# Two attention layers in one program: 64x64 tiles for the block layer's scores, norm scaling on GpSimd, sums of the full layer in halves

## What is computed

```python
# layer 1, block sparse: 16 blocks of 64 rows
q, k, v = (heads(x @ W.T + b) for each of Wq, Wk, Wv)
# block rows 0 and 15 attend to all 1024 keys; row 1 to blocks 0, 1, 2, 15; row 14 to 0, 13, 14, 15
# block rows i = 2..13 attend to blocks 0, i-1, i, i+1, 15
ctx = softmax(scores * scale) @ v
x = layernorm(x + ctx)
# layer 2, full attention, and a layer of 8 experts
hn = layernorm(x) * g1 + b1                  # q, k, v of hn; every row attends to all 1024 keys
x2 = x + (softmax(q @ k.T / sqrt(8)) @ v) @ wo + bo
hn2 = layernorm(x2) * g2 + b2
idx = argmax(hn2 @ gate_w + gate_b)          # one expert per row
x3 = x2 + (relu(hn2 @ w1[idx] + b1[idx]) @ w2[idx] + b2[idx])
out = layernorm(x + x3)
```

## Time and profile before

| what | us |
|---|---|
| median of 3 runs (lowest, highest) | 940.32 (936.14, 944.61) |
| the profiled execution's own time | 937.35 |
| its span, first to last instruction | 935.6 |
| TensorE busy | 762.3 |
| VectorE busy | 565.6 |
| ScalarE busy | 443.0 |
| GpSimd busy | 203.7 |

### The profile page before, as it was taken

The page is one execution under the profiler, slowest core; times in us unless marked ns, Lnnn a source line. Parts: engine busy times, 40 slices in busy tenths (PEclk is TensorE's granted clock), DMA queues, the critical chain, the costliest instruction groups (busy, mean ns, idle before and its releaser), DMA issues.

```text
span 935.6 us, 17249 instructions
## 1 busy us (share of the span) xinstructions
PE 762.3 (81%) x6594; PEld 343.4 (37%) x6594; DVE 565.6 (60%) x941; ACT 443.0 (47%) x826; POOL 203.7 (22%) x460
## 2 busy tenths in 40 slices
PE   4299999999999999977789999987999987305950
PEld 2135655556555565531122212131212122205950
DVE  3253344334554344579987899979789941623745
ACT  2024233333334334327767787866777886002621
POOL 5213420000223342011213410002100000063650
PEclk9557676658657776569989999999999999556985
DMA  4411111212111111111101111110111124013103
GB/s 120 67 18 19 19 19 19 26 19 30 19 19 19 19 19 19 19 15 18 17 10 17 18 22 22 26 14 11 16 18 20 18 78 126 0 40 87 34 32 90
DMA packets 28699, 28.88 MB, mean 31 GB/s; under 512 B 4592, under 2 KB 23824, under 8 KB 28624
## 3 DMA queue, kind: packets, MB, share of 16 engines
q1 hardware_dynamic: 27216, 24.96, 15.4%
q0 software_dynamic: 1408, 2.89, 0.9%
HBM read 9.35 MB, written 5.53 MB: 16 GB/s over the span
## 4 chain that ended last, share of the span: by engine, by line
PE 65%; DVE 18%; issue 5%; POOL 4%; ACT 4%; DMA 3%; SPq 1%; POOLq 0%; ACTq 0%; DVEq 0%
PE PO L1101 23%; PE RB L1138 22%; PE EX L1146 11%; DVE NM L874 11%; ACT PR L732 3%; PE EX L1058 2%; POOL sorted_rows L661 2%; PE RB L1190 1%; PE RB L1115 1%; POOL results L681 1%; PE EX L1197 1%; DVE ST L823 1%; DMA QKT<-QS 1%; PE RB L1089 1%; DVE X L843 1%
## 5 line engine op out<-in xcount | busy, mean ns | idle before, releaser
L874 DVE TENSOR_REDUCE NM<-RB 128x1 f32<-128x1024 f32 (+2 forms) x416 | 433.2, 1067 | 239.7 <-PE RB L1138 229.7
L732 ACT ACTIVATE PR<-EX 128x512 f32<-128x512 f32 (+1 forms) x736 | 383.1, 586 | 300.2 <-PE EX L1146 299.0
L1138 PE MATMUL RB<-QKT 48*128 48x512 bf16 (+4 forms) x1248 | 313.2, 339 | 55.8 <-DVE NM L874 35.5
L1146 PE MATMUL EX<-QKT 51*128 51x512 bf16 (+2 forms) x1536 | 305.6, 309 | 10.3 <-ACT PR L732 6.9
L1101 PE MATMUL PO<-PR,VB 128*32 128x512 f32 (+3 forms) x3072 | 253.1, 440 | 0.1
L1138 PEld LDWEIGHTS RB<-QKT 48*128 48x128 bf16 (+1 forms) x1248 | 94.0, 103 | 286.1 <-DVE NM L874 142.9
L1146 PEld LDWEIGHTS EX<-QKT 51*128 51x128 bf16 (+1 forms) x1536 | 99.4, 111 | 114.7 <-ACT PR L732 69.5
L1101 PEld LDWEIGHTS PO<-PR,VB 128*32 128x32 f32 x3072 | 94.6, 128 | 51.0 <-issue 35.8
L637 POOL COPY VB<-VST 128x128 f32<-128x128 f32 (+1 forms) x64 | 18.7, 292 | 340.4 <-PE PO L1101 327.7
L647 POOL CAST MS<-NM 128x16 bf16<-128x16 f32 x32 | 6.3, 198 | 169.3 <-DVE NM L874 142.0
L755 ACT COPY QS<-QS 128x1156 f32 x12 | 13.8, 1155 | 57.8 <-DVEq L965 43.1
(11 more groups left out here) (158 smaller groups left out, 510.7 us busy)
## 6 DMA issues: line engine op xcount, KB each, us to landing
QKT<-QS SPq DMA_DIRECT2D x64, 192.0 KB
QS<-in_L_ffn_w_dram SPq DMA_DIRECT2D x1, 2048.0 KB, 9.3
QS<-in_L_ffn_w_dram SPq DMA_DIRECT2D x4, 512.0 KB, 9.5
sorted_rows<-PR SPq DMA_DIRECT2D x3, 516.0 KB, 10.1
QKT<-sorted_rows SPq DMA_DIRECT2D x3, 516.0 KB, 5.6
QKT<-MT SPq DMA_DIRECT2D x64, 6.0 KB
CTX<-results SPq DMA_DIRECT2D x2, 512.0 KB, 5.1
X<-_attn_hidden_states_dram SPq DMA_DIRECT2D x2, 384.0 KB, 4.1
```

The lines of the kernel that those rows point to most:

```text
L732: nc.scalar.activation(PR[:, at % RING, h, 0:n], bank(key)[:, 0:n], ACT.Exp).then_inc(s_aread, 1)
L874: nc.vector.tensor_reduce(NM[v % 2][:, h, tiles[0]:tiles[-1] + 1], ps, AX_X, ALU.max, negate=True).then_inc(s_dread, 1)
L1138: ins = pe.matmul(spread(ps[r0:r1, c:c + of[1] * of[3]], of), columns(v, h, 0, ROWS6, (l0, 1, 0, ln)), columns(v, h, 1, ROWS6, of), start= ...
L1146: ins = pe.matmul(spread(ps[r0:r1, c:c + of[1] * of[3]], of), columns(xv, xh, 1, ROWS9, (l0, 1, 0, ln)), columns(xv, xh, 0, ROWS9, of), st ...
```

## The change

Four edits:
- In the block layer every score matmul that had a 128-column stationary operand becomes two of 64 columns, LOW and UPP, in both passes. The maxima's pieces are regrouped: `window` gives for each 64 rows the 128 columns of the outer blocks and then the near blocks, in one piece where they lie side by side.
- The last three AV groups of the block layer become one.
- In the full layer each AV group of 512 columns becomes two of 256, the first due one beat after its EXP step, the second (`late`) one more. Groups of the block layer are due at the later of the two.
- SCALE is done on GpSimd, in all norms but that of the second sequence ahead of the experts.

```diff
@@ full_layer
-    L.av_groups = [dict(last=2 * kt + 1,
-                        mms=[(h, a, 2 * kt + a, (0, 512), "full", kt, 0) for a in range(2) for h in range(2)])
-                   for kt in range(TT)]
+    L.av_groups = [dict(last=2 * kt + 1, late=half, mms=[(h, a, 2 * kt + a, (half * 256, 256), "full", kt, half * 256)
+                                                         for a in range(2) for h in range(2)])
+                   for kt in range(TT) for half in range(2)]
@@ block_layer
-    L.max_acts = [dict(tiles=(0,), n=1024, mms=[(ALL, k * 512, (0, P), (k * 512, 1, 0, 512)) for k in range(2)])]
+    def window(j, off, col):
+
+        blk, rows = 2 * j + off // BLK, UPP if off else LOW
+        query, c = (j * P + off, BLK), block_col(blk)
+        if j == TT - 1:
+            near = [(P, (block_col(13), 1, 0, P) if off == 0 else (block_col(2), 2, block_col(1) - block_col(2), BLK))]
+        elif block_col(blk - 1) == c - BLK:
+            near = [(P, (c - BLK, 1, 0, 3 * BLK))]
+        else:
+            near = [(P, (block_col(blk - 1), 1, 0, BLK)), (P + BLK, (c, 1, 0, 2 * BLK))]
+        return [(rows, col, query, (0, 1, 0, P))] + [(rows, col + c0, query, of) for c0, of in near]
+
+    def turns(f):
+
+        return [m for pair in zip_longest(f(0), f(BLK)) for m in pair if m]
+
+    L.max_acts = [dict(tiles=(0,), n=1024, mms=[(LOW if off == 0 else UPP, k * 512, (off, BLK), (k * 512, 1, 0, 512))
+                                                for k in range(2) for off in (0, BLK)])]
     for j in range(1, TT - 1, 2):
-        L.max_acts.append(dict(tiles=(j, j + 1), n=320, mms=[m for i in (0, 1) for m in [
-            (ALL, 512 * i, ((j + i) * P, P), (0, 2, (j + i) * P, P)),
-            (LOW, 512 * i + 2 * P, ((j + i) * P, BLK), (block_col(2 * (j + i) - 1), 1, 0, BLK)),
-            (UPP, 512 * i + 2 * P, ((j + i) * P + BLK, BLK), (block_col(2 * (j + i) + 2), 1, 0, BLK))]]))
+        L.max_acts.append(dict(tiles=(j, j + 1), n=320, mms=[m for i in (0, 1) for m in turns(
+            lambda off: window(j + i, off, 512 * i))]))
...
     L.exp_steps = [first[0], odd, first[1], even, own, rest, ends]
+    for st in L.exp_steps:
+        st["mms"] = [half for rows, c, (l0, ln), of in st["mms"] for half in
+                     ([(LOW, c, (l0, BLK), of), (UPP, c, (l0 + BLK, BLK), of)] if rows == ALL else [(rows, c, (l0, ln), of)])]
@@ plan
             for e in steps:
-                ready[e] = beats[i + 1] + 0.4
-        acts += [(ready[gr["last"]], 5, "AV", li, u, g) for g, gr in enumerate(L.av_groups)]
-        exp_end.append(ready[L.av_groups[-1]["last"]] + 0.2)
+                ready[e, 0], ready[e, 1] = beats[i + 1] + 0.4, beats[i + 2] + 0.4
+        acts += [(ready[gr["last"], gr.get("late", 1)], 5, "AV", li, u, g) for g, gr in enumerate(L.av_groups)]
+        exp_end.append(ready[L.av_groups[-1]["last"], 1] + 0.2)
@@ block.gpsimd
+                if kind == "SCALE" and (li, u) != (2, 1):
+                    src, dst = ((X, X1[:]), (X1, X[:]))[k[0]] if li == 1 else (X, HN2[:, :, 0:HS])
+                    for t in (2 * k[1], 2 * k[1] + 1):
+                        g = u * TT + t
+                        nc.gpsimd.tensor_scalar(dst[:, g, :], src[:, g, :], MV[:, t, 0:1], RD[:, t:t + 1],
+                                                ALU.subtract, ALU.mult).then_inc(s_norm, 1)
@@ block.vector
-                if kind == "SCALE":
-                    n, src, dst = 2 * u + k[0], (X, X1)[k[0]], (X1, X)[k[0]]
...
-                    if (li, u) != (2, 1):
-                        dve.wait_ge(s_newton, 4 * ROOT_STEPS * (n + 1))
-                    elif k[1] == 0:
+                if kind == "SCALE" and (li, u) == (2, 1):
+                    n = 4 + u
+                    if k[1] == 0:
```

More of the change, by code:

```diff
@@ L1 @@
 from contextlib import ExitStack
+from itertools import zip_longest
 import numpy as np
@@ L87, in block_layer @@
     t7 = (TT - 1) * P
-    L.max_acts = [dict(tiles=(0,), n=1024, mms=[(ALL, k * 512, (0, P), (k * 512, 1, 0, 512)) for k in range(2)])]
-    for j in range(1, TT - 1, 2):
-        L.max_acts.append(dict(tiles=(j, j + 1), n=320, mms=[m for i in (0, 1) for m in [
-            (ALL, 512 * i, ((j + i) * P, P), (0, 2, (j + i) * P, P)),
-            (LOW, 512 * i + 2 * P, ((j + i) * P, BLK), (block_col(2 * (j + i) - 1), 1, 0, BLK)),
-            (UPP, 512 * i + 2 * P, ((j + i) * P + BLK, BLK), (block_col(2 * (j + i) + 2), 1, 0, BLK))]]))
[L94 to L97, removed]
+    def window(j, off, col):
[12 more added lines that the diff above has]
+                                                for k in range(2) for off in (0, BLK)])]
+    for j in range(1, TT - 1, 2):
+        L.max_acts.append(dict(tiles=(j, j + 1), n=320, mms=[m for i in (0, 1) for m in turns(
+            lambda off: window(j + i, off, 512 * i))]))
+    L.max_acts.append(dict(tiles=(TT - 1,), n=256, mms=turns(lambda off: window(TT - 1, off, 0))))
     def single(j, col):
@@ L137, in block_layer @@
                                          (h, 0, 3, (0, 384), "full", 0, P)])),
[L138 to L143, removed]
+        dict(last=6, mms=both(lambda h: [(h, j % 2, 4, ((j - 1) * P, P), "full", j, j // 2 * P) for j in range(1, 5)]) +
+             both(lambda h: [(h, j % 2, 5, ((j - 5) * P, P), "full", j, j // 2 * P) for j in (5, 6)] +
+                  [x for a, b_ in ((1, 2), (3, 4))
+                   for pair in zip(single_v(h, 5, a, 2 * P + (a - 1) * BLK),
+                                   single_v(h, 5, b_, 2 * P + (b_ - 1) * BLK)) for x in pair]) +
+             both(lambda h: [x for pair in zip(single_v(h, 6, 5, 0), single_v(h, 6, 6, BLK)) for x in pair]))]
     L.kinds = ["full", "low", "upp"]
@@ L416, in av_group_of @@
         def av_group_of(li, e):
-            return [i for i, gr in enumerate(LAYERS[li].av_groups) if gr["last"] >= e][0]
+            return max(i for i, gr in enumerate(LAYERS[li].av_groups) if any(m[2] == e for m in gr["mms"]))
         def piece(li, b, k):
@@ L830, in do @@
                         root_guess(VE[:, 0:TT], RD[:, 0:TT], SD[:, 0:TT]).then_inc(s_var, 1)
-                if kind == "SCALE":
-                    n, src, dst = 2 * u + k[0], (X, X1)[k[0]], (X1, X)[k[0]]
-                    if li == 2:
-                        n, dst = 4 + u, HN2[:, :, 0:HS]
-                    if (li, u) != (2, 1):
-                        dve.wait_ge(s_newton, 4 * ROOT_STEPS * (n + 1))
-                    elif k[1] == 0:
+                if kind == "SCALE" and (li, u) == (2, 1):
+                    n = 4 + u
+                    if k[1] == 0:
                         dve.wait_ge(s_var, n + 1)
@@ L842, in do @@
                         g = u * TT + t
-                        nc.vector.tensor_scalar(dst[:, g, :], src[:, g, :], MV[:, t, 0:1], RD[:, t:t + 1],
+                        nc.vector.tensor_scalar(HN2[:, g, 0:HS], X[:, g, :], MV[:, t, 0:1], RD[:, t:t + 1],
                                                 ALU.subtract, ALU.mult).then_inc(s_norm, 1)
```

## The result

The changed kernel takes 844.14 us (median of 4 runs, 832.37 to 847.26) against 938.39 us before (4 runs); the ratio is 0.892 with a 95% interval of 0.879 to 0.904. Predicted were 863 us, 808 to 908. The profiled execution took 847.26 us with a span of 845.5. All ratios here leave out runs that count as slow: of the changed kernel 845.24 and the profiled 847.26, and elsewhere, among others, one run of the kernel before of 1377.76 us and two of e10 of 1802 us, which nothing here explains.

What follows compares the result with a forecast made beforehand. TensorE was taken to bound the block layer and VectorE the full layer. 937.35 - 64 (block layer units) - 3.5 (first unit) - 6 (scaling) = 863.9, said as 863 us, range 808 to 908.

Steps and rivals of the forecast that it cites:

- each turn costs: Block layer scores: full-width and half-width stationary shapes taking turns cost 0.22 us; ten turns are most of a 2.4 us beat.
- Halves run side by side: Block layer scores: low and high 64x64 halves overlap, 0.053 us for both together, at most some 0.026 a pair.
- Beats 3 and 4: Block layer, two maximum steps with exponent scores: 1.0 us each plus 0.4 for MT, 5.24 becomes 2.4, saving 2.8.
- Beats 5 to 8: Block layer: they wait for VectorE's reduces, 2.95 us to beat 9, where they and the sums took 4.61.
- over 16 units: Block layer: each unit falls from 20.9 to 16.9 us, 4.0 saved, 64 us over all 16 units.
- rival B: Block layer: denser stream raises the clock, units of about 12.5 to 13 us, 802 us in all; chance 0.20.
- C: Block layer: thin waits for VectorE lower the clock, 19.4 us a unit, 905 us in all; chance 0.17.
- I take 0: Full layer, sums by halves: 31 us of TensorE switches hidden behind reduces, net 0, bounds -10 to +31 us.
- Scaling, 6 us saved: Norms: 24 scalings in the full layer's time leave VectorE for GpSimd, 6 us saved, bounds 0 and 9.
- D: Full layer becomes TensorE's: the 31 us of switches land in full, 894 us; chance 0.06.
- E: Block layer: halves don't run side by side in long streams, columns double, about 940 us; chance 0.04.
- F: Block layer: 64-column weight loads come one after another, 0.11 us a pair, +4.9 us a unit, 1015 us; chance 0.05.

Runs made afterwards that it cites:

- e10: The kernel before with only the loads of q and k due 9 ahead of their unit in place of 6; 945.15 us, ratio 1.004.
- e1: The kernel before with the block layer's 64x64 score tiles alone, sums, due times and scaling as before; 876.74 us, ratio 0.934.
- e11: e5 with the block layer's maxima pieces as before the change (18 of 46 a unit with 128 columns), exponent's in 64x64; 912.25 us, ratio 0.975.
- e5: The changed kernel with the loads of q and k due 9 before their unit in place of 6; 820.38 us, beside 936.39 for the kernel before.
- e9: The changed kernel with the early loads and each block-layer score step's pieces ordered low halves first, then high ones; 816.36 us, ratio 0.868.
- e3: The kernel before with the full layer's sums in halves alone, due one beat and two after their exponents; 919.15 us, ratio 0.979.
- e2: The kernel before with the scaling of the norms moved to GpSimd alone; 927.96 us, ratio 0.990.
- e6: The changed kernel with the scaling of the norms back on VectorE; 854.65 us, ratio to before 0.912.

## Why the prediction was right, point by point

- Block layer, cost of the old form ("each turn costs"): right. e1 gives the whole gain and e11 takes it back. "Halves run side by side" was true too, and worth little: 0.1 to 0.2 us a beat (e5 against e9). The price of a pair, 0.026 us, was near: 29 pairs in 0.58 us and 41 in 0.87 are 0.020 and 0.021 us a pair at the high clock, 0.034 and 0.037 at the low one.
- Beats 3 and 4 at 1.0 us: beat 3 measured 1.0. Beats 5 to 8 with their waits for VectorE's reduces: some 3.1 us for 2.95, with beat 5 ahead of the big group of sums and not behind it, as the text had it. Merged sums 1.5: 1.53. A unit forecast at 16.9 measured 16.25 in the plain one shown.
- Yet the block stage gained 55 us for 67.5, and ended at 356 us and not near 342. The units between the first and the sixteenth copy of maxima gained what was forecast for them and more, 65 us for 60. The step that failed is "over 16 units": the last two units' exponents stand beside the full layer's 48*128 maxima, so for them the tiles brought the turns of shape in and did not take them out, 7.2 us lost by e1 and 11.5 in all where a unit's 4.0 were to be gained. The first unit's 3.5 came to 1.3.
- Two things that the sum left out went against each other inside the units. Beats of the next unit wait for the load of q and k, 26 us of new waits over the layer: the load's 8.7 us and its place behind the maxima's transfer in SyncE's list were never laid against the shorter unit. And the clock, taken as unchanged, rose from 0.66 to 0.74 between the same marks. With the loads early (e5) a unit there takes 15.7 us in the mean, and the stage is 83 us shorter than before.
- The clock: rival B took it to rise. It went from 0.65 to 0.70 over the block layer and to 0.76 in e5, where the two quickest units take 25.8 us, 12.9 each, the price that B had named; the mean stayed at 15.7. So B came in part. C (a falling clock) came in the last stretch alone, 0.61 to 0.54.
- Full layer, "I take 0" with bounds of -10 and 31: wrong in sign and outside the bounds, -22 by e3 alone. The step that failed is the reading of rows 6: 1.22 us is how long a reduce lasts, and I took it for VectorE's pace, so nothing was left to win in plain beats. Its pace is 1.13, as the rows of two show in the kernel before too, and the pace before was TensorE's 2.46 us for two. The beat itself was worked out rightly (1.10), and the mechanism stood in the text (the exponent's fourth piece no longer waits for its bank) without a price.
- Scaling, 6 us saved: 8 alone (e2), 11 on top of the rest (e6); right in kind, low in size: with the halves VectorE sets the pace, if only by 0.02 to 0.03 us a beat. GpSimd's row was bounded at 0.3 to 0.6 us and is 0.79; on an engine with that much idle time it cost nothing that shows.
- D, E and F didn't happen. F had a price of 0.11 us a pair; the runs show 0.020 to 0.037. The Trainium skill's TensorE: Matmul & The Clock Gate (LDWEIGHTS) prices a load at its columns / 1.2, an estimate of 53 ns for 64 columns, and the Trainium skill's TensorEngine Tiling (Array Packing) (Restrictions) says that column tiling turns the fast load off; neither bounds the pace of pairs here, 20 ns at the high clock. What the Trainium skill's TensorEngine Tiling (Array Packing) says of changes of tiling mode (Key Properties: a change drains the engine) agrees with e11, with 0.22 us a change in its timeline, lost overlap included.

So the range was met in part by luck: the sum came out at 863 for 844 because two misses went against each other, 12 us too much in the block layer and 28 and some too little in the full one.

## What to carry to other kernels

- Matmuls of different stationary shape that take turns cost far more than smaller ones of one shape: here 52 pairs more a unit went with 4 us less. Count the changes of shape first, and look also at the ends of a stage, where its matmuls stand beside those of the next: there the new shape was the one that didn't fit.
- When a stage gets a fifth shorter, lay every transfer and every queue's list against the new length, SyncE's too; here one number in the plan was worth 24 us after the change and nothing before it.
- How long an instruction lasts is not its pace. Take the shortest distance between starts in a row of many, and if an engine seems full, look whether the one that feeds it has a loop of the same length.

## What the runs showed of the hardware that I had not expected

- Back-to-back reduces of 1024 PSUM columns start 1.13 us apart though each lasts 1.22.
- GpSimd's 128x128 subtract-and-multiply with two pointers takes 0.79 us, where VectorE's takes 0.38 and GpSimd's own copy of that size 0.29.
- Pairs of load and matmul in 64x64 with mostly 64 to 192 columns pass at 0.020 to 0.021 us each at the high clock and 0.034 to 0.037 at the low one with low and high halves in turns; with the low halves first it is 0.024 to 0.025 and 0.042.
